# Node units that begin four steps behind the edge layers of block 0 in place of six

## The reference

```
h = maximum(layernorm(x), 0)
S = h[src]
msgs = where(rel == r, relu(relu(S @ W_rel[r].T + b_rel[r]) @ W_rel[r].T + b_rel[r]), msgs)   # r = 0, 1
agg = segment_sum(msgs, dst)
i, f, g, o = split(agg @ W_ih.T + b_ih + b_hh)
c = sigmoid(i) * tanh(g);  hn = sigmoid(o) * tanh(c)
y = relu(relu(hn @ W1.T + b1) @ W2.T + b2) @ W3.T + b3
out = x + y
```

## Time and profile before

| | |
|---|---|
| median of 3 runs | 2224.82 us (2221.1 to 2231.82) |
| the profiled execution | 2218.29 us, its span 2216.6 us |
| PE busy | 2052.0 us, 93% of the span |
| DVE, ACT, POOL busy | 81%, 79%, 55% |
| chain that ended last | PE 77%, issue 7%, DMA 5%, POOL 5% |

### The profile page before, as it was taken

One profiled execution on the slowest core, in us unless ns is written; L12 is line 12 of the kernel. 1 busy time (PEld: TensorE's weight loads), 2 busy tenths in 40 slices (PEclk: granted clock), 3 DMA queues, 4 the chain that ended last, 5 costly groups with the idle time before them and its releaser, 6 DMA issues.

```text
span 2216.6 us, 51618 instructions
## 1 busy us (share of the span) xinstructions
PE 2052.0 (93%) x13932; PEld 1374.4 (62%) x13933; DVE 1804.9 (81%) x4316; ACT 1759.4 (79%) x3811; POOL 1228.4 (55%) x917
## 2 busy tenths in 40 slices
PE   5868777777999999999999999999999999999996
PEld 4747565555666666666666666666666666445553
DVE  8757666556898989989898989898989987888886
ACT  3847555557999999999999999999999997666663
POOL 0057777777766666666666666676666634000000
PEclk7669888888999999999999999999999999999998
DMA  9975555557799999999999999999999989988886
GB/s 383 424 256 99 97 99 96 98 96 148 139 171 181 184 182 183 183 182 180 181 182 180 183 175 180 174 180 180 184 182 184 183 158 172 203 185 192 189 190 144
DMA packets 399983, 396.90 MB, mean 179 GB/s; under 512 B 263114, under 2 KB 342534, under 8 KB 393736
## 3 DMA queue, kind: packets, MB, share of 16 engines
q0 software_dynamic: 91200, 157.34, 44.3%
q1 hardware_dynamic: 305636, 238.11, 41.3%
q10 hardware_dynamic: 3044, 0.15, 0.1%
HBM read 185.89 MB, written 156.97 MB: 155 GB/s over the span
## 4 chain that ended last, share of the span: by engine, by line
PE 77%; issue 7%; DMA 5%; POOL 5%; DVE 3%; ACT 2%; POOLq 0%; DVEq 0%; ACTq 0%; SPq 0%
PE bank L1545 34%; PE bank L1492 9%; PE bank L1511 9%; PE bank L1584 6%; PE bank L1559 6%; PE bank L1528 4%; DMA agg<-summed,scatter_idx 4%; PE bank L1468 3%; PE bank L1568 3%; POOL agg L678 3%; POOL xg L662 2%; PE bank L1503 1%; DMA a_lo<-row_lo 1%; PE bank L1377 1%; PE bank L1405 1%
## 5 line engine op out<-in xcount | busy, mean ns | idle before, releaser
L678 POOL DMA_INDIRECT agg<-summed,scatter_idx x400 | 671.7, 1679 | 434.5 <-issue 203.4
L1545 PE MATMUL bank<-a_hi,ihT 128*128 128x512 f16 x2400 | 713.8, 379 | 2.8 <-DMA a_lo<-row_lo 2.4
L662 POOL DMA_INDIRECT xg<-in_x,src_ring x384 | 444.6, 1158 | 120.1 <-issue 120.1
L1545 PE MATMUL bank<-a_lo,ihT 128*128 128x512 f16 x1200 | 454.8, 379 | 0.0
L1545 PEld LDWEIGHTS bank<-a_hi,ihT 128*128 128x128 f16 x2400 | 234.5, 98 | 212.8 <-issue 2.6
L1511 PE MATMUL bank<-relT,h_hi 128*128 x1600 | 321.7, 275 | 0.0
L1492 PE MATMUL bank<-s_hi,relT 128*128 128x256 f16 x1600 | 301.6, 289 | 0.1
L686 POOL DMA_DIRECT2D y<-in_x x100 | 133.3, 1333 | 296.9 <-DVE y L1263 286.4
L1492 PE MATMUL bank<-s_lo,relT 128*128 128x256 f16 x800 | 231.1, 289 | 0.0
L799 ACT ACTIVATE xn<-xg,shift,rstd 128x256 f32<-128x256 f32 x400 | 218.3, 601 | 9.6 <-DVE shift L1177 9.6
L1511 PE MATMUL bank<-relT,h_lo 128*128 x800 | 220.1, 275 | 0.0
(11 more groups left out here) (205 smaller groups left out, 4726.5 us busy)
## 6 DMA issues: line engine op xcount, KB each, us to landing
agg_in<-agg SPq DMA_DIRECT2D x100, 512.0 KB
y<-in_x POOLq DMA_DIRECT2D x100, 512.0 KB, 8.2
out<-y SPq DMA_DIRECT2D x100, 512.0 KB, 8.0
agg<-zeros SPq DMA_DIRECT2D x24, 2112.0 KB, 16.1
dst_ring<-dst_rows SPq DMA_DIRECT2D x200, 128.0 KB
agg<-summed,scatter_idx POOLq DMA_INDIRECT x400
xg<-in_x,src_ring POOLq DMA_INDIRECT x384
src_ring<-src_slot SPq DMA_DIRECT2D x192, 1.0 KB
```

Of the source, the lines that this page charges most:

```text
L662: nc.gpsimd.indirect_dma_start(out=xg[:, k.slot(8), t, :], out_offset=None, in_=x[:, :], in_offset=bass.IndirectOffsetOnAxis(ap=rows[:, t: ...
L678: nc.gpsimd.indirect_dma_start(out=agg[:, :], out_offset=bass.IndirectOffsetOnAxis(ap=scatter_idx[:, k.slot(8), t:t + 1], axis=0), in_=sum ...
L1545: last = nc.tensor.matmul(N_C[c % 2][:, 0:UNIT], lhs, rhs, start=i == 0, stop=i == len(todo) - 1)
```

## The change

```
--- before.py
+++ after.py
@@ -102,7 +102,7 @@


 NB = QUARTER_PAIRS + 4
-N0 = NB + 6
+N0 = NB + 4
```

## The result

The changed kernel takes 2231.86 us (median of 20 runs, 2228.27 to 2233.07). The kernel before, run beside it, takes 2225.15 us (20 runs, 2221.09 to 2233.91). The ratio is 1.0024, with an interval of 1.0012 to 1.0035, so it costs 5.3 us (2.7 to 7.8), less than the 0.5% set as the bound; the two medians as they stand differ by 6.7 us. The forecast was +4.7 us.

The account below looks back on a forecast made before the run. The prediction took PE, full in the middle, as the bound, with POOL's scatters pacing the start. Its terms 7.9 - 8.8 + 1.3 + 0 + 4.3 summed to +4.7 us, 2229.5 us on the median, range 2217 to 2240 us.

Parts of the forecast that it names:

- the last scatters: Near the end: SP's wait for the last scatter delays unit 74's second transpose and PE's products, +4.3 us (2 to 6).
- ACT's tables: Start: square roots of step 58 between gates cost more table loads, and ACT comes late: +1.3 us (0 to 2.6).
- Edge work: Behind the first gate product, where PE is full: two more steps' edge work is left, +7.9 us.
- The first gate product: Start: it comes 8.8 us earlier despite SP's wait for the scatter of pair 51; bounds -4 to -10.5.
- ACT's way: Start: the other way to the first gate product, through unit 1's load and rounding, ready at 525.2 us, hidden behind 526.4.
- The middle: 70 loads in the middle: rows are there 4.7 us before ACT asks, so the later loads cost 0 us.
- rival B: Start: PE at the slower clock for the first 18 gate products, +3.9 us, sum +8.6 us, 2233.4 us; chance 0.13.
- Rival A: Both ends: waits hidden after all, 15.6 us go and 7.9 come back, -7.7 us, 2217 us; chance 0.12.
- Rival C: Middle: loads land later than ACT's rounding asks, slower by over 0.5%, +23 or +70 us; chance 0.09.
- D: Start: faster by over 0.5%, which needs POOL's pace to improve as well; chance 0.03.

Follow-up runs that it names:

- e1: The changed kernel with all units' rows loaded from x in place of agg, waiting for no scatter: 2216.79 us, ratio 0.9974.
- e11: The kernel before with node work starting two steps later (N0 = 62 in place of 60): 2234.34 us, ratio 1.0038.
- e12: The changed kernel again, unchanged, as control of the third set: 2237.49 us, ratio 1.0043.
- e9: The changed kernel with units 0 to 9 loaded from x without a wait for scatters: 2229.13 us, ratio 1.0012.
- e7: The changed kernel with unread matmuls put on PE ahead of its waits at steps 56 to 58 and 206: 2233.95 us, ratio 1.0025.
- after: The changed kernel itself, in its first measurement and trace: 2231.86 us, ratio 1.0024.
- e3: The changed kernel with every unit's load one step later, behind the next step's transposes: 2519.79 us, ratio 1.134.
- e10: The changed kernel with loads of units 1 to 3 and 75 behind the next step's transposes, ACT's roundings of 0 to 3 and 75 at step end: 2226.1 us.
- e6: The changed kernel with units 74 to 99 loaded from x without a wait for scatters: 2235.1 us, ratio 1.0037.
- e2: The kernel before (N0 = 60) with all units' rows loaded from x, waiting for no scatter: 2220.99 us, ratio 1.0.

## Why the prediction was right, step by step

The forecast of no change beyond 0.5%, on the slow side, holds in the first measurement; in the second (1.0043) the interval reaches 1.0062. Its structure holds too; two terms were too small: the last scatters for the clock alone, ACT's tables for the clock and by their own size.

- **Edge work, +7.9 us.** Shown: e1 loses 7.9 us at the place, e11 gains 7.9 us.
- **The first gate product, -8.8 us.** Measured -8.0 (e12: -6.1). The chain is the predicted one: scatter of pair 51, load, index loads, transposes, `a_lo`. From the start of that scatter's second half the second transpose goes out after 7.4 us (6.9 predicted) and lands in 4.61 (5.2). The bounds of this term, -4 and -10.5, don't follow from the landings given with them, 8.7 and 4.0 us; these give -5.3 and -10.0. e1 and e9 reach -12.8 and -13.1 without that wait, against 13.4 by POOL's pace. ACT's way, expected to hide behind it by 1.2 us, hid by less: the product follows the turning of pair 58 by 0.64 us of waiting.
- **ACT's tables, +1.3 us.** Measured with the clock 4.1 us until unit 12. Twelve products took 5.29 us in place of 2.59, so 2.7 us are clock by the rows. e7, at full clock behind its first gate product, loses 2.2 us, and e1, at full clock too, 2.9. The next wait of PE, for ACT's gates behind the table loads, is 0.93 us in `after`, 1.68 in e7 and 1.87 in e1: a slower PE waits less there. So tables and the late ACT are worth 2.2 to 2.9 us at full clock, and the clock adds some 1 to 2 us to that rather than its 2.7.
- **The middle, 0 us.** Confirmed: -3.9 at unit 12 and at unit 70. The loads come 1.9 us later in the median (0 to 3 were forecast), and ACT never waits for one there. e3 shows how near the edge it is.
- **The last scatters, +4.3 us.** The wait itself was sized right, 5.86 - 1.10 = 4.8 us, in part because two errors cancel: the last scatter landed 3.86 us after the start of its second half (1898.58 to 1902.44) where 5.5 were reckoned, and from the load to the second transpose it took 5.61 us where 3.7 were. Behind it came 6.93 - 3.88 = 3.0 us of low clock, which the term left out. Together 7.8 us by the rows; in the accounting 14.9 - 7.9 = 7.0.
- **The sum.** -8.0 + 4.1 + 0 + 7.9 + 7.0 = +11.0 us at unit 78. Behind it 1.5 us come back, where PE of the kernel before has small waits for `a_lo` of its own, and the end lies at +9.5. The ratios say 5.3 and, in the second measurement, 9.6 (the medians as they stand 6.7 and 10.3). The forecast, 4.7, left out the clock at both ends, 5.7 us by the rows. That it still lies 0.6 us from the first measurement is luck in part: the traces have it 4.8 us too low, and the execution of before that they are held against is itself 6.9 us below its median. Which of the two figures is nearer the truth, 5.3 or 9.6, isn't settled here.

**The step that was mis-sized** is thus the clock, and ACT's tables by another 0.9 to 1.6 us. The clock stood in the prediction as rival B, for the start only, at +3.9 us and a chance of 0.13, and was set aside because "before the change the same products ran at full clock right behind a stretch of waits". It happened at the start with 2.7 us, and at the last scatters, where nothing had been reckoned for it. What decides it isn't shown. After, PE waits 2.78 us for `xn` just ahead, then 0.64, and the clock falls; in the trace of before it waits 3.29 us for `m_lo` 2.7 us ahead of the same products, and they run at full clock. The Trainium skill ("TensorE: Matmul & The Clock Gate", "HAM oscillation") says that a TensorE that waits for a DMA between pieces of work goes on at half rate; the trace agrees near the last scatters, with a wait of 5.86 us for a DMA and a granted clock of 0.64 over 1914 to 1922 us. At the start the products take 0.44 us each in place of 0.216, but there the longer wait was for ACT. Not every wait brings it: behind e1's 1.92 us for `a_lo` two products take 0.59 us, the full rate, and behind e10's 2.78 us they take 1.01.

Rival A (waits hidden, -7.7 us) is refuted for the real kernel. e1, without the waits, is what it would look like: -5.8 us. Rival C is refuted for this change and shown to be real by e3, at 3 us per unit. D didn't come.

## What to carry to other kernels

Starting a second stage earlier moves work out of a stretch where the bound engine idles into one where it is full; the gain is the earlier start less all the work that was pushed across, here 13.4 less 7.9 us, before any new wait. On a queue that is worked in order, price a wait by all that stands behind it: in the middle the load had 5 us to spare and nothing was late, and at the two ends the transposes behind the wait were what PE waited for. To each wait of the bound engine add the low clock that can follow it, and try a remedy at the place of the wait alone, since the same edit in the loop body cost 3 us per iteration.

## What the runs showed of the hardware

- A wait of 5.86 us cost PE another 3.0 us in the eighteen products behind it, since the first of them ran at the 1.2 GHz level; with 24 matmuls put ahead of that wait, which left 2.44 us of it, they took 5.73 us, not 3.88 (e7).
- A load of 512 KB lands 7.8 us after its issue in the median where PE is busy all the time and the DMA share is 0.93 (e1), and 4.2 us where the share is 0.82 and the load stands at another place in the step (e3); POOL's addition of equal size takes 9.5 and 8.4 us in the same stretches. Which of the differences makes it is not shown.
- One DMA transpose landed 22.01 us after its issue in one execution (e6), 11.19 in another (e2), against 4.6 and 5.4 in `after`; in e6 the issue of the next transpose took 14.57 us, where the median of each trace is 1.3 to 1.5 us and the longest elsewhere 5.5 (e11). PE waited 18.07 and 14.03 us. Each kernel has one trace only, so it isn't shown that kernels whose loads wait for scatters are free of it. The cause is open.
